# Expert tiles as fp16 pairs, transposed in 32x32 blocks on VectorE

## What is computed

```python
x2d = hidden_states.reshape(T, D)                   # T = 2048 tokens, D = 512, after layernorm
router_logits = x2d @ gate_kernel                   # 32 experts
weights, selected = top_k(softmax(router_logits), 8)
weights = weights / sum(weights)
# rows sorted by expert, each expert's group of rows:
w0, w1 = rows @ gate_proj[e], rows @ up_proj[e]     # 512 x 192 each
expert_out = (silu(w0) * w1) @ down_proj[e]         # 192 x 512
output = sum over the 8 experts of a token, weighted
```

## Time and profile before

| | us |
|---|---|
| runs, median (lowest to highest) | 1493.65 (1492.18 to 1494.72) |
| profiled execution, span from first to last instruction | 1460.5 |
| PE busy | 1381.2 (95%) |
| DVE busy | 1028.4 (70%) |
| ACT busy | 505.4 (35%) |
| POOL busy | 382.6 (26%) |
| chain that ended last: PE | 76% |
| chain that ended last: DVE | 12% |

### The profile page before, as it was taken

One profiled execution on the slowest core, in us unless ns is written; L12 is line 12 of the kernel. 1 busy time (PEld: TensorE's weight loads), 2 busy tenths in 40 slices (PEclk: granted clock), 3 DMA queues, 4 the chain that ended last, 5 costly groups with the idle time before them and its releaser, 6 DMA issues.

```text
span 1460.5 us, 26973 instructions
## 1 busy us (share of the span) xinstructions
PE 1381.2 (95%) x7525; PEld 752.6 (52%) x7526; DVE 1028.4 (70%) x2471; ACT 505.4 (35%) x916; POOL 382.6 (26%) x313
## 2 busy tenths in 40 slices
PE   4799999999999999999999569999999999999997
PEld 3344444444444444455555246666665666656664
DVE  7879857975896555688887636666666666666664
ACT  0454544444344443432222123333333333333332
POOL 1000000000000000025556623434343344443443
PEclk9899999999999999999999779999999999999998
DMA  9975776767676778738768868899899898899786
GB/s 374 375 289 176 266 255 222 245 197 227 209 230 216 229 249 290 260 131 316 249 251 303 300 182 215 231 224 265 234 256 233 231 229 216 233 230 219 156 150 86
DMA packets 132696, 345.04 MB, mean 236 GB/s; under 512 B 15008, under 2 KB 19616, under 8 KB 125728
## 3 DMA queue, kind: packets, MB, share of 16 engines
q1 hardware_dynamic: 73488, 206.72, 41.9%
q0 software_dynamic: 34640, 85.74, 25.8%
q10 hardware_dynamic: 24512, 51.89, 11.1%
HBM read 192.68 MB, written 151.62 MB: 236 GB/s over the span
## 4 chain that ended last, share of the span: by engine, by line
PE 76%; DVE 12%; DMA 4%; issue 3%; ACT 2%; ACTq 1%; SPq 1%; POOLq 0%; DVEq 0%; POOL 0%
PE PS L1498 20%; PE PS L1500 19%; PE PS L1499 19%; PE PS L1731 5%; PE PS L1758 2%; PE PS L1757 2%; DMA split_experts<-HT 2%; PE PS L1746 1%; PE PS L1747 1%; PE PS L1641 1%; DVE HT L1051 1%; DMA X<-in_x 1%; ACTq L100 1%; DMA CST<-in_kv 1%; PE PS L1675 1%
## 5 line engine op out<-in xcount | busy, mean ns | idle before, releaser
L573 POOL DMA_INDIRECT out<-BIG,EX x159 | 247.1, 1554 | 362.7 <-issue 164.4
L1498 PE MATMUL PS<-BIG 128*128 x795 | 268.4, 338 | 6.0 <-DVE BIG L1401 4.6
L1499 PE MATMUL PS<-BIG 128*128 x795 | 268.4, 338 | 0.0
L1500 PE MATMUL PS<-BIG 128*128 x795 | 268.4, 338 | 0.0
L1498 PE MATMUL PS<-HT,BIG 128*128 128x512 f16 (+1 forms) x512 | 194.1, 379 | 2.9 <-DVE HT L1035 1.4
L1500 PE MATMUL PS<-HT,BIG 128*128 128x512 f16 (+1 forms) x512 | 194.0, 379 | 0.0
L1499 PE MATMUL PS<-HT,BIG 128*128 128x512 f16 (+1 forms) x512 | 194.0, 379 | 0.0
L551 POOL DMA_INDIRECT rows_by_expert<-HT,POS x128 | 124.1, 969 | 101.1 <-DVE POS L1298 66.7
L1498 PE MATMUL PS<-BIG,EX 128*128 128x512 f16 (+1 forms) x384 | 146.5, 382 | 3.0 <-DVE EX L1240 3.0
L1500 PE MATMUL PS<-BIG,EX 128*128 128x512 f16 (+1 forms) x384 | 146.8, 382 | 0.0
L1499 PE MATMUL PS<-BIG,EX 128*128 128x512 f16 (+1 forms) x384 | 146.6, 382 | 0.0
(11 more groups left out here) (243 smaller groups left out, 2226.1 us busy)
## 6 DMA issues: line engine op xcount, KB each, us to landing
BIG<-rows_by_expert ACTq DMA_DIRECT2D x159, 280.0 KB, 5.6
HT<-in_experts SPq DMA_DIRECT2D x64, 640.0 KB, 4.6
BIG<-split_experts SPq DMA_DIRECT2D x32, 1152.0 KB
split_experts<-HT SPq DMA_DIRECT2D x96, 320.0 KB, 2.3
CST<-in_kv SPq DMA_DIRECT2D x64, 256.0 KB, 4.7
split_context<-RT SPq DMA_DIRECT2D x64, 256.0 KB, 4.5
BIG<-split_context SPq DMA_DIRECT2D x7, 2048.0 KB, 13.3
rows_by_expert<-X SPq DMA_DIRECT2D x32, 280.0 KB, 7.8
```

Of the source, the lines that this page charges most:

```text
L573: pool.indirect_dma_start(a_out, bass.IndirectOffsetOnAxis(ap=IDY[:, u % V:u % V + 1], axis=0), yt[u % V], None, compute_op=ALU.add).then_ ...
L1498: mm(out, lh, rh, start=first, stop=False)
L1499: mm(out, lh, rl, start=False, stop=False)
L1500: return mm(out, ll, rh, start=False, stop=last_group)
```

## The change

Rows are now kept in DRAM as pairs of fp16 values, high and low, in the place of each fp32 value. In the attention stage the normalised tile goes to one fp32 buffer `rn`; ACT writes its high halves and DVE its low halves into the slot that is scattered (`pack_hi`, `pack_lo`). In the expert stage a row load becomes five DMAs: four, each filling 32 partitions with a quarter of the row's columns, as four pieces of 512 bytes for each partition, and one for the 48 words behind the values (`tail`). DVE then transposes the tile in 32x32 blocks, straight into interleaved pairs `xT`, which PE reads as stationary operand with a step of two. TensorE's row transposes, `tile_hi` and `tile_lo` go. What was ACT's wait for the weights in `tile_hi` stays as a wait and an increment of a semaphore (`weights_here`), for which `tile_up` waits. PE's hidden transpose moves behind the first three matmuls of the gate/up product. On the host the rows of the gate and up weights are put in the order that the new transpose yields. The diff, cut ("..."):

```diff
 V = U
+LANDED = 16 * 5
...
+        rn = SUMX[:, KC * P:KC * P + D]
...
+        ZP = HT[:, 4096:4096 + ZN * RW].bitcast(F16).rearrange("p (z w h) -> p z w h", z=ZN, h=2)[:, :, 0:D, :]
...
-        xg = [BIG[:, o + i * RW:o + (i + 1) * RW] for i in range(U)]
-        ids = [row[:, C_ID:C_ID + 1].bitcast(I32) for row in xg]
-        o += U * RW
+        xg = [BIG[:, o + i * D:o + (i + 1) * D] for i in range(U)]
+        o += U * D
+        tail = [BIG[:, o + i * (RW - D):o + (i + 1) * (RW - D)] for i in range(U)]
+        ids = [row[:, C_ID - D:C_ID - D + 1].bitcast(I32) for row in tail]
+        o += U * (RW - D)
...
-        xh = [f16(BIG, o + i * D // 2, (KC, P)) for i in range(2)]
-        xl = [f16(BIG, o + D + i * D // 2, (KC, P)) for i in range(2)]
+        xT = [BIG[:, o + i * D:o + (i + 1) * D] for i in range(2)]
+        pair = [x.bitcast(F16).rearrange("p (k n h) -> p k n h", k=KC, h=2) for x in xT]
...
+            def pack_hi(t):
+                act.wait_ge(s_nr, t + 1)
+                act.activation(ZP[:, t % ZN, :, 0], rn, ACT.Copy, scale=H_S).then_inc(s_here, 1)
...
+                    pack_hi(t - 1)
                     router_hi(t - 1)
...
-            def tile_hi(t, p, weights):
-                act.wait_ge(s_wl, weights)
-                act.wait_ge(s_xt, t + 1)
-                act.activation(xh[p], PS[:, p, :].rearrange("p (k n) -> p k n", n=P), ACT.Copy, scale=H_S).then_inc(s_xh, 1)
+            def weights_here(weights):
+                wait_apart(act, s_wl, weights, s_here)
...
-                act.dma_start(xg[u], d_row[bass.ds(row, P), :]).then_inc(s_xg[u], 16)
+                rows = d_row[bass.ds(row, P), :]
+                for q in range(4):
+                    act.dma_start(xg[u][q * 32:(q + 1) * 32, :].rearrange("i (b w) -> i b w", b=4),
+                                  rows[:, q * P:(q + 1) * P].rearrange("(b i) w -> i b w", b=4)).then_inc(s_xg[u], 16)
+                act.dma_start(tail[u], rows[:, D:RW]).then_inc(s_xg[u], 16)
...
-                    tile_hi(t + 2, u % 2, due[u + 2])
+                    weights_here(due[u + 2])
                     load_tile((u + LEAD) % U, t + (V + LEAD - U + 1), rows[u + LEAD - 4], due[u + LEAD])
                     tile_silu(t + 1, (u + 1) % 2)
...
+            def pack_lo(t):
+                dve.wait_ge(s_here, t + 1)
+                v.scalar_tensor_tensor(ZP[:, t % ZN, :, 1], rn, H_S, ZP[:, t % ZN, :, 0],
+                                       ALU.mult, ALU.subtract).then_inc(s_pk, 1)
...
+                dve.wait_ge(s_pk, t + 1)
...
-                    tile_normalise(ZR[:, (t - 1) % ZN, 0:D], t - 1, 0).then_inc(s_nr, 1)
+                    tile_normalise(rn, t - 1, 0).then_inc(s_nr, 1)
...
+                    pack_lo(t - 1)
                     router_lo(t - 1)
                     choose(t - 1)
...
-            def tile_lo(t, p):
-                dve.wait_ge(s_xh, t + 1)
-                v.scalar_tensor_tensor(xl[p], PS[:, p, :].rearrange("p (k n) -> p k n", n=P), H_S, xh[p],
-                                       ALU.mult, ALU.subtract).then_inc(s_xl, 1)
+            def tile_transpose(t, u, n):
+                dve.wait_ge(s_xg[u], n * LANDED + LANDED)
+                v.transpose(xT[u % 2].rearrange("p (c b i) -> p b c i", c=KC, b=4),
+                            xg[u].rearrange("p (b c j) -> p b c j", b=4, c=KC)).then_inc(s_xt, 1)
...
-                v.tensor_scalar(yt[u % V], PS[:, 5 + u % 2, :], xg[u][:, bass.ds(e + D, 1)], None, ALU.mult).then_inc(s_y, 1)
...
-                    tile_lo(t + 2, u % 2)
+                    tile_transpose(t + 2, (u + 2) % U, it + (u + 2) // U)
                     hidden(t + 1, (u + 1) % 2)
                     weigh(t, u, it * (U // V) + u // V, experts[u])
...
-                transpose_tile(ZR[:, t % ZN, 0:D], s_rt)
+                transpose_tile(rn, s_rt)
...
-            def tile_transpose(t, u, n):
-                pe.wait_ge(s_xg[u], n * 16 + 16)
-                for k in range(KC):
-                    last = nc.tensor.transpose(PS[:, u % 2, k * P:(k + 1) * P], xg[u][:, k * P:(k + 1) * P], ident[:, :])
-                last.then_inc(s_xt, 1)
...
-            def tile_up(t, p, at):
+            def tile_up(t, p, at, between=()):
+                pe.wait_ge(s_here, t + (NT + 1))
+                pe.wait_ge(s_xt, t + 1)
                 for k in range(KC):
                     hi = we[:, bass.ds(at + k * GU, GU)]
                     lo = we[:, bass.ds(at + (EW + k * GU), GU)]
-                    last = three(PS[:, 2 + p, 0:GU], xh[p][:, k, :], xl[p][:, k, :], hi, lo, k == 0, k == KC - 1)
+                    last = three(PS[:, 2 + p, 0:GU], pair[p][:, k, :, 0], pair[p][:, k, :, 1], hi, lo, k == 0, k == KC - 1)
+                    if k == 0:
+                        for due, q in between:
+                            pe.wait_ge(s_ea, due)
+                            hidden_transpose(q)
                 last.then_inc(s_ug, 1)
...
-            tile_transpose(0, 0, 0)
-            tile_transpose(1, 1, 0)
-            pe.wait_ge(s_xl, 1)
             tile_up(0, 0, weights_at("first_weights", 0, 4)[0])
             with pe.Fori(0, LOOPS) as it:
                 at = weights_at("tile_weights", it * U, U + 4)
                 for u in range(U):
                     t = it * U + u
-                    tile_transpose(t + 2, (u + 2) % U, it + (u + 2) // U)
-                    pe.wait_ge(s_ea, t + 1)
-                    hidden_transpose(u % 2)
-                    tile_up(t + 1, (u + 1) % 2, at[u + 1])
+                    tile_up(t + 1, (u + 1) % 2, at[u + 1], [(t + 1, u % 2)])
                     tile_down(t, u % 2, at[u])
...
-    gu = np.reshape(np.transpose(np.reshape(gu, (NE, KC, P, 2 * M)), (0, 2, 1, 3)), (NE, P, KC * 2 * M))
+    gu = np.reshape(np.transpose(np.reshape(gu, (NE, 4, KC, P // 4, 2 * M)), (0, 1, 3, 2, 4)), (NE, P, KC * 2 * M))
```

More of the change, by code:

```diff
@@ L337, in build @@
         s_add = [sem(f"tile_added{i}") for i in range(V)]
-        s_xt, s_xh, s_xl, s_ug, s_es, s_ea, s_at, s_ah2, s_al2, s_ed, s_y = (sem(n) for n in (
-            "tile_transposed", "tile_hi", "tile_lo", "tile_gate_up", "tile_silu", "tile_hidden", "hidden_transposed",
+        s_pk, s_here, s_xt, s_ug, s_es, s_ea, s_at, s_ah2, s_al2, s_ed, s_y = (sem(n) for n in (
+            "row_lo_packed", "row_hi_packed_then_weights_here", "tile_transposed", "tile_gate_up", "tile_silu", "tile_hidden", "hidden_transposed",
             "hidden_t_hi", "hidden_t_lo", "tile_down", "tile_weighted"))
@@ L821, in _ @@
                 load_tile(t, 0, rows[t], due[t])
-            tile_hi(0, 0, due[0])
-            tile_hi(1, 1, due[1])
+            weights_here(due[0])
+            weights_here(due[1])
             tile_silu(0, 0)
@@ L838, in _ @@
                 if u + 2 < REST:
-                    tile_hi(t + u + 2, u % 2, due[u])
+                    weights_here(due[u])
                 if u + LEAD < REST:
@@ L1413, in weigh @@
                 v.tensor_copy(IDY[:, u % V:u % V + 1], ids[u])
-                v.tensor_scalar(yt[u % V], PS[:, 5 + u % 2, :], xg[u][:, bass.ds(e + D, 1)], None, ALU.mult).then_inc(s_y, 1)
-            tile_lo(0, 0)
-            tile_lo(1, 1)
+                v.tensor_scalar(yt[u % V], PS[:, 5 + u % 2, :], tail[u][:, bass.ds(e, 1)], None, ALU.mult).then_inc(s_y, 1)
+            tile_transpose(0, 0, 0)
+            tile_transpose(1, 1, 0)
             hidden(0, 0)
@@ L1431, in _ @@
                 if u + 2 < REST:
-                    tile_lo(t + 2, u % 2)
+                    tile_transpose(t + 2, (u + 2) % U, LOOPS + (u + 2) // U)
                 if u + 1 < REST:
@@ L1777, in _ @@
                 t = LOOPS * U + u
-                if u + 2 < REST:
-                    tile_transpose(t + 2, (u + 2) % U, LOOPS + (u + 2) // U)
-                pe.wait_ge(s_ea, t + 1)
-                hidden_transpose(u % 2)
                 if u + 1 < REST:
-                    tile_up(t + 1, (u + 1) % 2, at[u + 1])
+                    tile_up(t + 1, (u + 1) % 2, at[u + 1], [(t + 1, u % 2)])
+                else:
+                    pe.wait_ge(s_ea, t + 1)
+                    hidden_transpose(u % 2)
                 tile_down(t, u % 2, at[u])
```

## The result

The changed kernel takes 1604.6 us (median of four runs, 1603.7 to 1614.2) where the kernel before takes 1494.2 beside it: ratio 1.0752, interval 1.0731 to 1.0773. That is slower by 110 us; forecast were 1588 and +95, within 1500 to 1655. The profiled execution's span is 1602.3 us.

A forecast was written before the change was run, and what follows sets the result against it. PE bounded the kernel before; ACT's chain of 4.08 us a tile was to bound the changed one. Expert stage +81, its start +9 and attention +5 made +95 on the median 1493.65: 1588 us, range 1500 to 1655.

The forecast's parts named there:

- What bounds the kernel; PE's work: Expert stage: PE bounds at 3.69 us a tile; without the row transposes (0.44) it needs 3.25.
- The block of five issues: ACT, between hidden_hi and silu: five load issues 0.515 us apart hold the sequencer 2.40 us; silu starts 0.04 later.
- The chain: Expert stage, hidden transpose to hidden transpose through ACT's issues and silu: 4.08 us a tile, above PE's 3.25.
- Turns: Eight-tile loop's turns: ACT's integer loads, now exposed, cost 1.4 us each, 27 us over nineteen; range nothing to 27.
- Stage, start, attention: Expert stage +81 us (667 against 586), its start +9 from 30 issues, attention stage +5 from packing (0 to 11).
- What lies around the span: Whole run: 33 us between profiled span 1460.5 and median 1493.65 lie around the span and don't change.
- DVE: Expert stage: the 32x32-block transpose takes 0.69 us, as tile_lo did, with 1.2 us to spare before silu starts.
- DMA: Expert-stage loads: 720 packets a tile at 36 ns, 25.8 engine-us; whole demand 4.06 us a tile, an upper value, hidden.
- (a): Expert stage: the issues do not hold silu or cost little, PE stays the bound; 1439 us, chance 0.10.
- (b): ACT's queue: five issues come 0.37 us apart, block 1.82, period 3.50; 1500 us, chance 0.08.
- (c): Expert stage: DMA engines become the bound at 43 ns a packet, 4.38 us a tile; 1635 us, chance 0.12.
- (d): Loop turns: PE idles 2.2 us and its clock halves, a tile then taking 6.5 us; 1634 us, chance 0.10.

The follow-up runs named there:

- the packing alone: Kernel before with only the change's attention part, expert stage left old (output meaningless): 1463.3 us, ratio 1.0012.
- the run with two issues: Changed kernel with each tile's load as one DMA of whole rows plus the tail, two issues for five (wrong element order): 1411.5 us in the profiled execution.
- five long issues: Changed kernel with its four quarter DMAs each taking 32 whole rows of 2048 B, plus the tail (wrong element order): 1571.2 us, ratio 1.0751.
- the split: Changed kernel with two of five load issues ahead of silu and three behind: 1496.7 us, ratio 1.0012; again in another set 1466.5, ratio 1.0036.
- narrowed kernel before: Kernel before, loading fewer integers per loop turn (ACT 8 and 12 for 12 and 16, starting two further on; PE 9 for 12): 1548.1 us, ratio 1.0594.

## Why the prediction was right

**What bounds the kernel; PE's work.** Right. With the issues out of the way the period was 3.25 to the hundredth, which is also what PE's matmuls took before, so that the interleaved halves as stationary operand cost it no time.

**The block of five issues.** Right: 2.36 us for 2.40, with 0.10 in place of 0.04 behind it. The choice between a pitch of 0.515 and 0.37 was the step on which all hung. Four issues in 1.77 to 1.85 us are 0.48 to 0.51 apart, so the neighbours whose address comes from a register were the ones to go by. On ACT in the first loads (880.90 to 896.25) the 30 issues took 15.4 us, forecast 15.3.

**The chain.** 4.14 us in the tile shown, 4.08 forecast: 0.06 more from transpose to hidden_hi, 0.06 more behind the issues, 0.04 less for these and 0.02 less ahead of them. The mean of the tiles that are at no turn is larger, 4.24. Of those 133 periods 22 are over 4.5 us and the others average 4.11. In most of the 22 ACT's issues themselves take longer, five in 3.0 us on average where the others have 2.34. In 19 of them SP issues a DMA of padding rows (L495) for an expert; it does so in only 7 of the other 111. The longest (5.71, at 1249.27):

```profile
1250.03 2.76 ACTq L825 DMA_DIRECT2D BIG<-rows_by_expert  x4
...
1250.43 0.34 SPq L495 DMA_DIRECT2D rows_by_expert<-X  x1
```

Four issues then take 2.76 in place of 1.8; another 0.67 lies there between silu and the next hidden transpose. Whether SP's issue or the transfer behind it slows ACT's isn't separated. The sum left such tiles out. Eight places at 4.08 and a turn of 1.4 make 34.0 us, measured 35.2; nineteen of these differences are 22 us of the stage, some 5 of them the 0.03 by which the ordinary tile is over 4.08, some 19 the late tiles, less 2 at the turns.

**Turns.** Right: the first place after a turn has 5.52 on average, 1.28 over the others, 24 us for the forecast 27. The timeline shows silu at 1075.57 and hidden_hi at 1078.01, 2.44 apart where a tile has 1.39.

**Stage, start, attention.** The stage +99.9 for +81 (22 us as above, less 3 for the transpose missed in the earlier trace rows), the start +9.1 for +9, the attention stage +2.4 for +5 (the packing alone, within its noise): 111.4 together, and the timed runs say 110.4. The error of the forecast is the tile's term: its mean was 4.24 in place of 4.08, most of it the late tiles, for which the sum had no term.

**What lies around the span.** Wrong, without effect. The 33 us between the profiled span of 1460.5 and the median of 1493.65 don't lie around the span; the span of 1602.3 stands beside 1604.1 for that same execution, and that of 1409.6 in the run with two issues beside its own 1411.5. So about 2 us lie around it. The rest is the longer attention stage, which the timed runs of the kernel before had and its profiled execution had not. The +95 was added to the median of the timed runs, so nothing of this went into the forecast.

**DVE.** Right: the transpose takes 0.70 us (159 of 701 ns mean) for 0.69. By the 311 ns for 128x128 bf16 of the Trainium skill, "VectorE: DVE Perf Modes", section "The three transpose paths", the estimate was 1.24 us; the measurement, of 4-byte elements, decides.

**DMA.** The upper value was too high. In 1100 to 1200 the ACT queue's 15776 packets, 21.9 tiles of 720, took 26.6% of 1600 engine-us: 27 ns each and 19.4 us a tile, for 25.8 put as an upper value and 14.0 before. The whole-run shares of that queue say the same: between five long issues (12.0% of 16 engines in 1566.6 us) and the change (13.5% in 1602.3) lie 61056 packets and 453 engine-us, 7 ns for each additional packet.

**The rivals.** (a) Issues cost little: excluded by the trace of after and the split. (b) Pitch 0.37: excluded, 0.48 to 0.51. (c) DMA engines the bound: its sign, DVE's transpose waiting for a DMA, doesn't show behind the first two tiles, and it is excluded by the five long issues and by the split, whose DMA share of 1.02 goes with a period of 3.25. By the rule of the Trainium skill, "SBUF — State Buffer", section on Door 1, a tile's load would have doubled from 14.0 to 28 engine-us (which makes 67, not the 68 of the prediction, in a tile's demand); measured were 19.4, with small packets among the causes, so the doubling isn't seen here. Five long issues, also of 32 partitions each, took 22.9% for 7328 packets, 21.8 tiles: 16.8 us. (d) The clock: it stays at 1.00 from the first hidden transpose of the profiled change to the last; it did fall with idle of 2.3 us in one piece in the narrowed kernel before. At the changed kernel's turns PE's idle time comes in shorter pieces (0.47, 0.61 and 0.89 us at this one):

```profile
1070.00:1075.00 5.00, 3.79 (x22) 1.93 (x20) 2.25 (x6) 0.71 (x2) 0.68 (x1) 1.00 1.03 302
1075.00:1080.00 5.00, 3.90 (x21) 1.87 (x20) 2.25 (x6) 0.71 (x2) 1.25 (x1) 1.00 0.81 188
```

## What to carry to other kernels

A DMA issue isn't free for the engine that issues it: count its time (here about half a microsecond) on that engine's queue, and look at which instruction stands behind it and who waits for that. Before taking up or dropping a change that splits a load, try another place for its issues: here the same five cost 7.5% ahead of silu and 0.1 to 0.4% when spread over both of the engine's gaps. What an edit takes off the busiest engine is gained only if the other chains are shorter than the new period; and a load of fewer integers can be slower, so change its start and its size one at a time.

## What was not expected of the hardware

- Integers loaded into registers on ACT: 12 in 0.79 us from a start at a multiple of four, in 2.60 us from a start two further on, nineteen turns of the two slower loads and the clock's falls costing 87 us. The kernel before's loads behind its last turn are slow too: 5 integers on ACT from a start at 154 took 1.86 us, and 7 on DVE from 152, a multiple of four, took 1.69, where its loads of 8 take 0.60 at most turns. So the number can count as well as the start; which numbers are slow no run sorts out.
- A DMA share of 1.00 to 1.02 of the 16 engines didn't mean that transfers were late: two issues and the split ran at PE's 3.25 us with it, where the kernel before had 0.90 at 3.69. A share near one is no proof of a bound.
- Packets of 512 B were cheap as additional ones: 7 ns of one engine each.
- The same kernel file has an attention stage of 191 us in one set of runs and 225 in another, which moves every time here from 1461 to 1496. In the trace of after nine evictions of the router's logits wait 30.0 us in all for a release shown as "remote", in the traces of the shorter kind none does. What causes it stays open. One of them:

```profile
704.68 0.19 DVE L1287 TENSOR_SCALAR RT<-PS 128x32 f32<-128x32 f32 x1 [2.67 <-remote]
```
